# Weights and first tiles of four stages loaded during the stage before, and one attention's first group loaded in halves

## The reference, cut to what matters

```python
def reference(...):
    # L0_attn: causal attention, 16 heads of 16, one slope per head (alibi)
    x = x + attention(layernorm(x) @ W_attn + b_attn) @ W_proj + b_proj
    # L0_ffn: two layers (DEPTH = 2), each of them
    h = shift_token(z)                       # second half of the channels moved down by one token
    q, k, v = split(h @ wqkv); q = l2norm(q) * q_scale; k = l2norm(k) * k_scale
    q, k = rotary_xpos(q, k)                 # tables of cos, sin and scale by position
    z = z + local_attention(q, k, v) @ wo    # 8 heads of 64, window of 128
    h = layernorm(shift_token(z)) * ln_g + ln_b
    a, g = split(h @ w1 + b1)
    z = z + (a * gelu(g)) @ w2 + b2
    # L1_attn: a state space layer (projections, a convolution of 4 taps, a scan)
    # L1_ffn: a mixture of 32 experts
```

## Time and profile before

| | us |
|---|---|
| median of 3 runs | 3671.98 |
| the runs | 3669.59 to 3672.42 |
| the profiled execution, whole | 3675.01 |
| its span, first to last instruction | 3673.2 |

### The profile page before, as it was taken

How to read it: one execution, slowest core, us unless ns; L and a number is a source line. 1 busy time by engine, 2 the same in 40 slices (tenths; PEclk the granted TensorE clock), 3 DMA queues, 4 the chain that set the end, 5 groups by cost and what they waited for, 6 DMA issues and landing times. The chain is left out here.

```text
span 3673.2 us, 52297 instructions
## 1 busy us (share of the span) xinstructions
PE 3235.6 (88%) x18096; PEld 1975.8 (54%) x18096; DVE 2455.5 (67%) x4653; ACT 1849.0 (50%) x3943; POOL 1432.4 (39%) x993
## 2 busy tenths in 40 slices
PE   8599999879999799799999799798288888887798
PEld 4244444346666555466666455333256565655676
DVE  8488888547777422277777232398599999996633
ACT  2176776736666411166666211355377777774100
POOL 4101111122222211122222111134599999996533
PEclk9699999989999899899999899899699999999899
DMA  5956575120000241100000321343525151512873
GB/s 170 150 68 92 80 96 79 34 67 25 23 23 23 91 145 46 58 23 23 23 23 20 94 69 46 96 152 144 212 83 201 58 201 58 201 58 88 294 229 118
DMA packets 275715, 347.29 MB, mean 95 GB/s; under 512 B 70976, under 2 KB 206640, under 8 KB 274812
## 3 DMA queue, kind: packets, MB, share of 16 engines
q1 hardware_dynamic: 259596, 305.70, 30.5%
q10 hardware_dynamic: 10736, 25.94, 2.0%
q0 software_dynamic: 5120, 12.30, 0.9%
HBM read 227.72 MB, written 112.80 MB: 93 GB/s over the span
## 5 line engine op out<-in xcount | busy, mean ns | idle before, releaser
L2414 POOL TENSOR_TENSOR H_feed<-H_ndu,H_bs 128x1024 f32<-128x1024 f32 x256 | 595.6, 2372 | 7.0 <-DMA H_cs<-between_bc 4.0
L852 ACT ACTIVATE B_probs<-B_p_exp,B_key_bias 128x512 f32<-128x512 f32 (+3 forms) x768 | 394.8, 583 | 143.2 <-PE B_p_exp L910 112.8
L750 DVE TENSOR_REDUCE B_part_max<-B_p_max 128x1 f32<-128x512 f32 (+3 forms) x768 | 374.7, 546 | 83.3 <-PE B_p_max L874 80.8
L1286 ACT ACTIVATE D_probs<-D_scores,D_neg,D_rq 128x256 f32<-128x256 f32 x512 | 283.1, 573 | 255.7 <-DVE D_neg L1198 255.7
L2385 ACT ACTIVATE H_decay<-H_ndt,H_rate 128x1024 f32<-128x1024 f32 x256 | 287.9, 1125 | 198.7 <-DVE H_turning L2467 103.1
L871 PE MATMUL B_p_max<-B_k,B_q 100*128 100x512 bf16 (+3 forms) x768 | 256.7, 341 | 43.8 <-DMA B_key_bias<-in_key_bias 33.7
L1696 PE MATMUL E_p_ag<-E_hT,E_w 128*128 128x512 f32 x640 | 282.8, 601 | 2.1 <-ACT E_hT L1652 2.1
L2467 DVE TENSOR_TENSOR_SCAN H_turning<-H_decay,H_feed 128x1024 f32<-128x1024 f32 x112 | 253.5, 2275 | 22.9 <-POOL H_feed L2414 22.7
L2518 PEld LDWEIGHTS H_p_y<-H_minus,H_sT 128*128 128x128 f32 x1792 | 225.1, 200 | 75.6 <-ACT H_sT L2370 55.6
L2518 PE MATMUL H_p_y<-H_minus,H_sT 128*128 128x128 f32 x1792 | 233.5, 287 | 35.8 <-ACT H_sT L2370 35.8
L907 PE MATMUL B_p_exp<-B_q,B_k 100*128 100x512 bf16 (+3 forms) x768 | 250.1, 329 | 11.4 <-ACT B_probs L852 6.5
(11 more groups left out here) (269 smaller groups left out, 6857.8 us busy)
## 6 DMA issues: line engine op xcount, KB each, us to landing
H_bs<-between_bc SPq DMA_DIRECT2D x64, 512.0 KB, 7.7
H_cs<-between_bc SPq DMA_DIRECT2D x36, 512.0 KB, 8.4
B_q<-between_q_parts SPq DMA_DIRECT2D x96, 128.0 KB
B_k<-between_k_parts SPq DMA_DIRECT2D x96, 128.0 KB
between_slots_x<-E_clear ACTq DMA_DIRECT2D x4, 2570.0 KB
I_xe<-between_slots_x ACTq DMA_DIRECT2D x32, 257.0 KB, 4.0
D_base<-between_z SPq DMA_DIRECT2D x64, 128.0 KB
between_z<-D_z SPq DMA_DIRECT2D x64, 128.0 KB
```

The lines of the kernel that those rows point to most:

```text
L750: nc.vector.reduce_max(part_max[:, g % 2, kc, qb, h:h + 1], p_max[:, use % 3, 0:keys], AX.X).then_inc(maxed, 1)
L852: nc.scalar.activation(probs[:, x % PROBS, skip:512], p_exp[:, n % SCORES, skip:512], ACT.Exp, bias=key_bias[:, g % SETS, kb - 4 * Q + 4, ...
L1286: last = nc.scalar.activation(probs[:, place[m], :, :].rearrange("p a b -> p (a b)"), scores[:, place[m], :, :].rearrange("p a b -> p (a b ...
L2414: nc.gpsimd.tensor_tensor(feed[:, n % AHEAD, :], ndu[:, g % 2, :], bs[:, s, :], ALU.mult).then_inc(fed, 1)
```

## The change

Two classes own the tiles and semaphores of the local attentions (LocalAhead) and of the feed forwards (FeedAhead) that are loaded ahead. They outlive the stages. LocalAhead.load issues 17 transfers (11 on one semaphore, and tiles 0 to 2), FeedAhead.load 24 (18 on one semaphore, and chunks 0 and 1), all on SP's queue:

- local.load for layer 0 in attention, in the turn of group 10, after put_shift(11); for layer 1 in the feed forward of layer 0, after the store of chunk 3.
- feed.load in each local attention, after the store of tile 16.

In the local attention GpSimd multiplies only block 0 of rope ahead of the masks, and blocks 2i + 1 and 2i + 2 after inverses(i). In the feed forward the zeroing of the 5140 columns moves from the start to behind the first inverse deviation; every engine waits once, for all weights. In attention, group 0 is loaded in halves of 512 tokens, q on SP's queue and k on ScalarE's; TensorE waits for the first half (14 transfers) and, at its 17th product, for the second (12). In the front, dt_b is negated on GpSimd, and ScalarE waits for it only ahead of its first put_xs.

```diff
@@ phase_attention
+            def load_first():
+                for half, done in ((0, first_half), (1, second_half)):
+                    cols = slice(512 * half, 512 * half + 512)
+                    for n, part in enumerate((0, 0, 1, 1, 0, 2)):
+                        sp.dma_start(q[HD * n:HD * n + HD, 0, :, cols], T["q_parts"][part_rows(0, part), cols]
+                                     .rearrange("(h d) t -> d h t", h=GH)).then_inc(done, 16)
+                    if half == 0:
+                        sp.dma_start(q[96:KR, 0, :, :], T["q_rows"]).then_inc(done, 16)
+                values(0)
...
-            load(0)
+            load_first()
             load(1)
             load(2)
             put_shift(0)
...
+                if g == NG - 6:
+                    sp.wait_ge(first_row, 16)
+                    sp.wait_ge(z_stored[0], 16)
+                    local.load(sp, T, 0)
...
         @block.scalar
         def _(act):
+            for half, done in ((0, first_half), (1, second_half)):
...
+                    act.dma_start(k[HD * n:HD * n + HD, 0, :, cols], T["k_parts"][part_rows(0, part), cols]
+                                  .rearrange("(h d) t -> d h t", h=GH)).then_inc(done, 16)
...
+                if n == 0:
+                    pe.wait_ge(first_half, 16 * 14)
+                if g == 0 and qb == QB // 2 and kc == 0 and h == 0:
+                    pe.wait_ge(second_half, 16 * 12)
@@ phase_window
+                if i == TILES // 2:
+                    sp.wait_ge(first_row, 16)
+                    for u in range(2):
+                        sp.wait_ge(stored[u], 16 * 4)
+                    feed.load(sp, T, layer)
...
-            pool.wait_ge(ident_loaded, 16)
-            pool.wait_ge(band_loaded, 16)
+            pool.wait_ge(local.weights, WEIGHTS)
+            tables(0)
             pool.drain()
...
-            pool.wait_ge(rope_loaded, 16 * 7)
-            for b in range(BLOCKS):
-                nc.gpsimd.tensor_tensor(rope[:, b, :, :], rope[:, b, :, :], factor[:, :, :], ALU.mult
-                                        ).then_inc(rope_ready, 1)
...
             for i in range(TILES):
                 inverses(i)
+                for b in range(2 * i + 1, min(2 * i + 3, BLOCKS)):
+                    tables(b)
@@ phase_feed_forward
             load_rest(0)
             load_rest(1)
...
+                if i == 3 and not last_layer:
+                    sp.wait_ge(stored[0], 16)
+                    local.load(sp, T, layer + 1)
...
-            if not last_layer:
-                nc.gpsimd.memset(clear[:, :], 0.0).then_inc(clear_ready, 1)
             for i in range(CHUNKS):
...
                 nc.gpsimd.tensor_tensor(rstd[:, u, :], spread[:, :], power[:, :], ALU.pow).then_inc(rstd_ready, 1)
                 if i == 0:
-                    pool.wait_ge(b2_loaded, 16 * CT)
+                    if not last_layer:
+                        nc.gpsimd.memset(clear[:, :], 0.0).then_inc(clear_ready, 1)
+                    pool.wait_ge(feed.weights, WEIGHTS)
                 pool.wait_ge(rest_loaded[u], 16 * rest_transfers * (i // 2 + 1))
                 last = nc.gpsimd.tensor_tensor(rest[:, u, :, :], rest[:, u, :, :], b2[:, :, :], ALU.add)
@@ phase_front
+            nc.gpsimd.tensor_scalar(dt_b[:, :], dt_b[:, :], -1.0, None, ALU.mult).then_inc(bias_ready, 1)
...
             def put_xs(k):
+                if k == 0:
+                    act.wait_ge(bias_ready, 1)
...
-            act.wait_ge(small_loaded, 16 * (TAPS + 3 + XT))
-            nc.scalar.mul(dt_b[:, :], dt_b[:, :], -1.0).then_inc(bias_ready, 1)
-            act.wait_ge(bias_ready, 1)
             put_xT(0)
@@ LocalAhead.load (17 transfers)
+        sp.dma_start(self.ident[:, :], T["ident"][:, :]).then_inc(self.weights, 16)
...
+        sp.dma_start(self.wo[:, :, :], T["wo"][layer].rearrange("(k p) n -> p k n", p=P)).then_inc(self.weights, 16)
+        for i in range(3):
+            self.load_tile(sp, T, i)
```

## The result

The changed kernel took 3634.21 us (median of 4 runs, 3633.56 to 3635.47) beside 3671.09 us for the kernel before (4 runs, 3669.59 to 3672.42): 36.9 us less, ratio 0.9896, 95% interval 0.9880 to 0.9911. The forecast was 3628.5 with a range of 3612 to 3645. The profiled executions give 3675.01 and 3633.56 us, with spans of 3673.2 and 3631.7, 41.5 us apart; the profiled run of before stood some 4 us above its median.

A forecast was written before the change was run, and what follows sets the result against it. Chains of loads and small steps at stage starts, not a busy engine, were taken as the bound. Terms 15.5 + 15 + 0.3 + 7.9 + 4.8 + 5.5 - 5.5 gave 43.5 us off, median 3628.5 us, range 3612 to 3645.

The forecast's parts named there:

- start of D, layer 0: Layer 0's local attention start: loads already landed 8.3, fewer tables before the norm 6.4, high clock 0.8; 15.5 us off.
- start of D, layer 1: Layer 1's local attention start: 8.0 us off from the loads, the rest as in layer 0; 15 us off.
- start of E, layer 0: Layer 0's feed forward start: statistics 6.5 us earlier, but GpSimd's zeroing and addition hold normalise 6.2; 0.3 us off.
- start of E, layer 1: Layer 1's feed forward start: statistics 6.2 us earlier, TensorE's 1.7 us wait for chunk 1 gone; 7.9 us off.
- start of F: Front's start: ScalarE copies the first transposes without waiting behind small weights and dt_b; 4.8 us off.
- start of B: Attention's start: group 0 in halves brings the exponential products forward, limited by put_shift(0) behind load(2); 5.5 us off.
- load ahead in B: Attention, group 11: 17 extra transfers delay load(14) and the yT stores, so the projection waits; 5.5 us lost.
- other loads ahead: Loads issued ahead during local attention and feed forward: covered by slack, cost nothing; some 5 us a place without cover.
- it then lies behind load(2)'s tail and lands at about 169.3: Attention's start: put_shift(0), issued after load(2) at 163.9, lands at 169.3; exponential products start then, 5.5 us off.
- the fourth rival: Attention's start gives all 9 to 11 us or nothing: 3624 or 3634 us; chance 0.06.
- the load of tile 20 is needed a tile and a half later: Local attention: SP is away 15 us for 24 transfers, a tile takes 16 us, so this costs nothing.
- The 0.8 us for a high clock at the scores: Local attention's tile 0: TensorE, at work earlier, reaches the high clock by the scores; 0.8 us off.

The follow-up runs named there:

- e1: Changed kernel with group 0's four shift transfers issued by ScalarE behind its copy, not by SP behind load(2): 3632.47 us, ratio to before 0.9880.
- e2: Changed kernel with SP issuing group 0's shift transfers before load(2) and not after it: 3623.64 us, ratio to before 0.9852.
- e12: Changed kernel with shift transfers ahead of load(2) and group 0 loaded whole by SP, as before the change: 3632.37 us, ratio to before 0.9884.
- e9: Changed kernel with GpSimd making all 8 tables at the start of a local attention again: 3642.61 us, ratio to before 0.9907.
- e4: Changed kernel with layer 0's feed forward zeroing waiting until VectorE has normalised chunk 0: 3627.49 us, ratio to before 0.9869.
- e6: Changed kernel with the zeroing left beside normalise, but GpSimd's addition waiting until normalise is done: 3630.88 us (one run).
- e7: Changed kernel with attention's load ahead moved from behind group 11's shift transfers to behind group 14's: 3632.86 us, ratio to before 0.9882.
- e5: Changed kernel with the zeroing back at the start of layer 0's feed forward, tiles already loaded: 3636.26 us (one run).
- e8: Changed kernel with the feed forward's 24 load-ahead transfers issued three at a time behind tiles 16 to 23: 3637.10 us, ratio to before 0.9891.
- e11: The changed kernel itself measured once more, nothing edited: 3632.35 us, ratio to before 0.9884.
- e3: Changed kernel with group 0's halves all issued by SP, q and k in turn, none by ScalarE: 3640.59 us, ratio to before 0.9907.

## Why the prediction was right, and where it was not

The time was right to 5.7 us; of the eight terms six held. Part of it is luck: 4.2 us missing at attention's start, 1.7 at tile 18 and 0.8 of the load ahead stand against 3.4 us that no term had. The table adds up to the 41.5 us between the two profiled executions, the forecast's 43.5; the medians are only 36.9 apart, because the profiled execution of before stood 3.9 us above its median and that of after 0.7 below.

| term | forecast | measured | by |
|---|---|---|---|
| start of D, layer 0 | -15.5 | -15.1 | start to first yT, 42.2 to 27.1 |
| start of D, layer 1 | -15.0 | -16.4 | the same, 43.5 to 27.1 |
| start of E, layer 0 | -0.3 | -0.5 | start to transposes, 11.6 to 11.1 |
| start of E, layer 1 | -7.9 | -8.0 | transposes -6.3, chunk 1's wait -1.7 |
| start of F | -4.8 | -4.8 | start to the expansion, 17.0 to 12.2 |
| start of B | -5.5 | -1.3 | to exp |
| load ahead in B | +5.5 | +6.3 | the two intervals |
| other loads ahead | 0 | +1.7 | tile 18 of layer 0 |
| clock and the rest | 0 | -3.4 | below |

**The step that failed** is "it then lies behind load(2)'s tail and lands at about 169.3". All before it came earlier than forecast: the first product at 130.2 (133), the maxima's end at 154.0 (158.5), the issue at 160.2 (163.9). The transfers were waited for 13.3 us after their issue, not the 5.4 that I gave them. I had sized the wait by what was left of load(2)'s bytes. e1 shows that it isn't a matter of that queue, and e2 that it is one of what has been issued before them. The chain had got rid of a 14 us wait for data and taken on a 12.5 us longer one for four small transfers; what came is nearest to the fourth rival's "nothing" (3634).

**A cover that was thinner than I wrote**: "the load of tile 20 is needed a tile and a half later". The row of 24 held SP for 19.4 us, not for 15, since one of its transfers took 5.3 us to issue; it held up tile 19's load as well, and TensorE waited 1.88 us for it, in some kernels and layers and not in others. The end of the cover was priced at some 5 us a place; it was 0 to 1.7, and once 6.0 (e12).

**Right for a reason that was only half right**: the start of the local attentions. The two parts were booked as if they added, 8.3 for the loads and 6.4 for the tables. e9 shows the tables' part at 2.4 to 3.6, since GpSimd, with its factors there at the start, has over half of its 5.5 us behind it before the norm is ready; with the loads alone the first yT came 11.6 and 13.2 us earlier than in the kernel before. The sum doesn't depend on it; the value of either part alone does. The 0.8 us for a high clock at the scores were wrong: they took 3.66 us, at the low level as before.

**Right as reasoned**: the zeroing (6.05 us lost of the 6.2 that the nearest row gave; e4 to e6), the wait at the projection of group 11 (4.29 and 1.8 for its slow products, forecast 5.5; e7 takes both away; the 19.5 us that the forecast gave to load(14) and the residual chunk are 20.5 by its own rows, 559.5 to 580, which would have made it 6.5), chunk 1's wait in layer 1, and the front.

**What no term had** is the clock outside tile 0. It is worth 1 to 2.4 us a place either way: the first expansion took 19.00 us for 19.88 in layer 0 and 20.03 for 18.88 in layer 1, and near the front's end the same eight products took 3.70 us for 6.06. The stretches (columns as in the earlier trace rows), the kernel before and then the changed one, the same 10 us of the work:

```profile
2540.00:2550.00 10.00, 7.83 (x12) 2.88 (x12) 9.85 (x7) 6.24 (x8) 6.10 (x2) 0.66 0.18 63
```

```profile
2501.60:2511.60 10.00, 9.49 (x25) 3.47 (x25) 9.85 (x7) 8.02 (x11) 6.13 (x2) 1.00 0.33 120
```

2.4 of the front's 6.8 us are this, and they are not the change's: with the same front, e2, e5, e8, e9, e11 and e12 show a granted clock of 0.66 at that place and 314.7 to 315.8 us for the stage, the six other edits 1.00 and 312.6 to 313.5.

## What to carry to other kernels

A small transfer that everything waits for should be issued before the bulk loads that nobody needs yet: here its queue made no difference (e1), and what had been issued before it made 9.4 us (e2). When loads are brought forward, look at the next step of the same chain, and put the loads ahead where no periodic load or store follows them; the same 4.1 MB cost 1.2 to 11.2 us in one place and nothing three groups later. A long row of issues on one queue holds up what that queue serves next, by anything from 0 to 6.0 us here; in small portions it cost nothing. Work moved behind an engine's first result may start in the very instant in which its neighbour begins on that result, and hold it up; one wait on the neighbour's semaphore gave back 5 us.

## What the runs showed of the hardware that I had not expected

- Four transfers of 8 KB, issued from ScalarE's empty queue while SP's transfers filled the engines, moved 7 to 14 us later and were waited for until 16.5 us after the first issue (156.29 to 172.83); into empty engines they took 3.9 us.
- Two queues side by side moved the first tiles faster than one: 1.97 MB from 120 to 132 us against 1.48 MB from 121 to 133. Two stretches of the DMA view, the changed kernel and then e3:

```profile
q1 hardware_dynamic: 1944, 1.15, 54.5%
q10 hardware_dynamic: 968, 0.82, 38.3%
```

```profile
q1 hardware_dynamic: 1918, 1.48, 50.1%
```

- The same code of attention took 625.9 to 638.1 us in the profiles of seven kernels (the changed kernel itself 632.7 and 625.9), mostly by the two waits for transfers in full engines; the tiles of local attention take 14.88 us within 0.1 us in all kernels, but for the waits told of, the last tile and a few that take 0.2 or 0.35 more at the same place each time.
